# Conditioned linear attention: two bias sums in column groups, another bank for one key product, and another order of the first loads

## The reference

```python
xn = _ln(x, ln_w, ln_b)
q = xn @ Wq + bq
k = xn @ Wk + bk + (1.0 - src_mask) * -1000000.0
q = softmax(q.reshape(b, t, h, dh), axis=-1)      # h = 8 heads of dh = 64
k = softmax(k.reshape(b, t, h, dh), axis=1)       # over the tokens
v = ((xn @ Wv + bv) * src_mask).reshape(b, t, h, dh)
att = einsum('bnhd,bnhl->bhdl', k, v)
y = einsum('bnhd,bhdl->bnhl', q, att).reshape(b, t, d)
scale, shift = split(silu(emb) @ W_emb + b_emb)
hh = _ln(y, ln2_w, ln2_b) * (1.0 + scale) + shift
return x + silu(hh) @ W_out + b_out
```

## Time and profile before

| | us |
|---|---|
| median of 3 runs | 471.26 (470.62 to 471.79) |
| the profiled execution | 471.46 |
| its span, first to last instruction | 469.5 |
| PE busy | 459.6 (98%) |
| DVE busy | 347.2 (74%) |
| ACT busy | 255.7 (54%) |
| POOL busy | 133.8 (28%) |

### The profile page before, as it was taken

How to read it: one execution, slowest core, us unless ns; L and a number is a source line. 1 busy time by engine, 2 the same in 40 slices (tenths; PEclk the granted TensorE clock), 3 DMA queues, 4 the chain that set the end, 5 groups by cost and what they waited for, 6 DMA issues and landing times.

```text
span 469.5 us, 7280 instructions
## 1 busy us (share of the span) xinstructions
PE 459.6 (98%) x2486; PEld 375.0 (80%) x2486; DVE 347.2 (74%) x844; ACT 255.7 (54%) x471; POOL 133.8 (28%) x149
## 2 busy tenths in 40 slices
PE   4999999999999999999999999999999999999997
PEld 3678877886888878888888888888878868888886
DVE  6768947776987947879768667676999827886852
ACT  5524322331878533347655555566799923766771
POOL 0413310221110000104323222225300032786685
PEclk9999999999999999999999999999999999999999
DMA  7936401111233201110212130312232032343322
GB/s 268 379 115 238 167 2 46 45 45 57 100 100 112 96 9 45 47 45 1 67 46 90 53 113 18 134 66 72 98 108 88 0 109 73 114 134 114 112 91 89
DMA packets 23187, 43.49 MB, mean 93 GB/s; under 512 B 1960, under 2 KB 2288, under 8 KB 23152
## 3 DMA queue, kind: packets, MB, share of 16 engines
q1 hardware_dynamic: 22592, 41.98, 26.0%
q10 hardware_dynamic: 560, 1.05, 0.6%
HBM read 34.64 MB, written 8.39 MB: 92 GB/s over the span
## 4 chain that ended last, share of the span: by engine, by line
PE 97%; DVE 1%; DMA 1%; ACT 0%; issue 0%; DVEq 0%
PE ps L1237 25%; PE ps L1239 25%; PE ps L1238 25%; PE ps L1242 10%; PE ps L1419 6%; PE ps L1341 2%; PE ps L1305 1%; PE ps L1397 1%; PE ps L1313 1%; PE ps L1262 1%; PE ps L1297 1%; DMA x_in<-in_x_dram 1%; PE ps L1401 0%; PE ps L1320 0%; ACT x_in L352 0%
## 5 line engine op out<-in xcount | busy, mean ns | idle before, releaser
L623 POOL TENSOR_TENSOR qs<-qs,qmax 128x512 f32<-128x512 f32 x32 | 36.1, 1130 | 172.0 <-DVE qmax L829 172.0
L1237 PE MATMUL ps<-wq_hi,zT_hi 128*128 128x512 f32 x128 | 52.2, 408 | 0.0
L1237 PE MATMUL ps<-wk_hi,zT_hi 128*128 128x512 f32 x124 | 51.1, 412 | 1.0 <-DVE kf L810 1.0
L338 ACT ACTIVATE zT_hi<-ps 128x512 fp32r<-128x512 f32 x32 | 19.1, 596 | 60.0 <-PE ps L1242 60.0
L1237 PE MATMUL ps<-ek_hi,zm_hi 128*128 128x512 f32 x128 | 50.4, 393 | 0.0
L1239 PE MATMUL ps<-wq_hi,zT_lo 128*128 128x512 f32 x128 | 50.2, 392 | 0.0
L1238 PE MATMUL ps<-wq_lo,zT_hi 128*128 128x512 f32 x128 | 49.9, 390 | 0.0
L1239 PE MATMUL ps<-ek_hi,zm_lo 128*128 128x512 f32 x128 | 49.9, 390 | 0.0
L1238 PE MATMUL ps<-ek_lo,zm_hi 128*128 128x512 f32 x128 | 49.8, 389 | 0.0
L1239 PE MATMUL ps<-wk_hi,zT_lo 128*128 128x512 f32 x124 | 48.7, 393 | 0.0
L1238 PE MATMUL ps<-wk_lo,zT_hi 128*128 128x512 f32 x124 | 48.3, 390 | 0.0
(11 more groups left out here) (250 smaller groups left out, 1156.8 us busy)
## 6 DMA issues: line engine op xcount, KB each, us to landing
x_in<-in_x_dram SPq DMA_DIRECT2D x35, 512.0 KB, 3.6
res<-in_x_dram SPq DMA_DIRECT2D x24, 256.0 KB, 2.8
out_dram<-res SPq DMA_DIRECT2D x24, 256.0 KB, 2.0
out_dram<-x_in SPq DMA_DIRECT2D x7, 256.0 KB, 2.0
y<-in_L_cond_Wk_dram ACTq DMA_DIRECT2D x2, 512.0 KB, 4.4
kf<-in_L_cond_Wq_dram SPq DMA_DIRECT2D x1, 1024.0 KB, 6.3
eq<-in_L_cond_W_out_dram SPq DMA_DIRECT2D x1, 1024.0 KB, 8.3
wv_mod<-in_L_cond_Wv_dram SPq DMA_DIRECT2D x1, 1024.0 KB, 10.5
```

The lines of the kernel that those rows point to most:

```text
L338: act.activation(o, i, ACT.Copy, scale=scale).then_inc(s[done], 1)
L623: pool.tensor_tensor(q_heads, q_heads, qmax[:, n % 2, :].unsqueeze(2).broadcast_to([P, H, DH]), ALU.subtract).then_inc(s["q_shift"], 1)
L1237: pe.matmul(o, a[0], bb[0], start=start, stop=False)
```

## The change

Three edits. The bias sums of query and value are formed as four matmuls with 32 columns of weights, each into its own 32 partitions of bank YTB, one per block (`bias_parts`); ScalarE copies that bank to `bias_part` in SBUF; one full matmul with `part`, a 128x128 matrix of 1/32, sums the parts and spreads them on all partitions (`bias_sum`), into bank YB + 1. The query's parts are formed ahead of `product_q(0, 0)` and summed behind it, the value's are formed in step 7 and summed in step 8. The key product of tile 15 of the first batch goes to bank OB, and the state's first products in banks 0 and 3 wait for all 16 key sums. ScalarE requests the first half of wk ahead of ln_w and ln_b.

```diff
-        bv_all = kf[:, 14, :]
+        bias_part, bv_all = kf[:, 15, :], kf[:, 14, :]
...
+            def load_wk(half):
+                act.dma_start(wk_raw[:, 2 * half:2 * half + 2, :],
+                              wk.rearrange("(c p) n -> p c n", p=P)[:, 2 * half:2 * half + 2, :]).then_inc(s[f"wk_in{half}"], 16)
+
+            load_wk(0)
             for v, at in ((ln_w, LNW), (ln_b, LNB)):
                 act.dma_start(ln_rows[at:at + NB, :], v.rearrange("(c p) -> c p", p=P)).then_inc(s["ln_in"], 16)
-            for half in range(2):
-                act.dma_start(wk_raw[:, 2 * half:2 * half + 2, :],
-                              wk.rearrange("(c p) n -> p c n", p=P)[:, 2 * half:2 * half + 2, :]).then_inc(s[f"wk_in{half}"], 16)
+            load_wk(1)
...
                 copy(wq_scaled[:, f, :], wq_raw[:, f, :], "wq_scaled", ln_weight(f))
+            act.wait_ge(s["bq_part"], 1)
+            copy(bias_part, ps[:, YTB, :], "bq_copy")
             normalise_x(0, 2)
             normalise_x(0, 3)
             for n in range(T):
                 if 2 <= n + 1 < T:
                     zT_high(0, n + 1)
+                if n == 8:
+                    act.wait_ge(s["bv_part"], 1)
+                    copy(bias_part, ps[:, YTB, :], "bv_copy")
...
-                dve.scalar_tensor_tensor(out=kf[:, n, :], in0=ps[:, OB if m == 1 else KB, :], scalar=pen[:, m:m + 1],
+                dve.scalar_tensor_tensor(out=kf[:, n, :], in0=ps[:, OB if m in (1, T - 1) else KB, :], scalar=pen[:, m:m + 1],
...
-            dve.tensor_tensor(bq_all[:], bq_all[:], ps[:, YTB, :], ALU.add).then_inc(s["bq_ok"], 1)
+            dve.tensor_tensor(bq_all[:], bq_all[:], ps[:, YB + 1, :], ALU.add).then_inc(s["bq_ok"], 1)
...
-                if m >= 2:
+                if m == T - 1:
+                    pe.wait_ge(s["k_sum"], 2)
+                elif m >= 2:
                     pe.wait_ge(s["k_sum"], m if m > 2 else 1)
...
-            def bias_sum(bank, by, raw, done):
+            def bias_parts(bank, by, raw, done):
 
                 for f in range(NB):
-                    last = pe.matmul(ps[:, bank, :], by[:, f:f + 1].broadcast_to([P, P]), raw[:, f, :],
-                                     start=(f == 0), stop=(f == NB - 1))
+                    last = pe.matmul(ps[32 * f:32 * f + 32, bank, :], by[:, f:f + 1].broadcast_to([P, 32]), raw[:, f, :],
+                                     start=True, stop=True)
                 last.then_inc(s[done], 1)
+
+            def bias_sum(bank, parts, done):
+                pe.matmul(ps[:, bank, :], part[:], parts, start=True, stop=True).then_inc(s[done], 1)
...
+                    if n == 0 and j in (0, 3) and b == 0:
+
+                        pe.wait_ge(s["k_sum"], T)
...
             pe.wait_ge(s["wq_in"], 16)
+            bias_parts(YTB, cols[:, LNB:LNB + NB], wq_raw, "bq_part")
             product_q(0, 0)
-            bias_sum(YTB, cols[:, LNB:LNB + NB], wq_raw, "bq_ps")
+            pe.wait_ge(s["bq_copy"], 1)
+            pe.wait_ge(s["part_ok"], 1)
+            pe.wait_ge(s["cols_ok"], 2)
+            bias_sum(YB + 1, bias_part, "bq_ps")
...
                     pe.wait_ge(s["wv_in"], 16)
-                    pe.wait_ge(s["cols_ok"], 2)
-                    bias_sum(YB + 1, lnb_w, wv_mod, "bv_ps")
+                    bias_parts(YTB, lnb_w, wv_mod, "bv_part")
+                if n == 8:
+                    pe.wait_ge(s["bv_copy"], 1)
+                    bias_sum(YB + 1, bias_part, "bv_ps")
```

More of the change, by code:

```diff
@@ L204, in cond_linear_attention @@
         names = """table_ok ln_in vec_in wk_in0 wk_in1 wq_in wv_in wo_in bk_in bq_in bias_in ident0 ident_ok part_ok ones_ok pick_ok
-            vec_ps cols_ok lnbw_ok kb_ps bq_ps bv_ps bk_ok bq_ok row_ok
+            vec_ps cols_ok lnbw_ok kb_ps bq_part bq_copy bq_ps bv_part bv_copy bv_ps bk_ok bq_ok row_ok
             wk_hi_ok wk_lo_ok wq_hi_ok wq_scaled wq_lo_ok wv_ok wo_hi_ok wo_lo_ok
@@ L1271, in product_k @@
                 for f in range(NB if m else 0):
-                    last = split_product(ps[:, OB if m == 1 else KB, :], (zT_hi[:, n % 2, f, :], zT_lo[:, n % 2, f, :]),
+                    last = split_product(ps[:, OB if m in (1, T - 1) else KB, :], (zT_hi[:, n % 2, f, :], zT_lo[:, n % 2, f, :]),
                                          (wk_hi[:, f, :], wk_lo[:, f, :]), f == 0, f == NB - 1)
```

## The result

| | before | changed kernel |
|---|---|---|
| median of timed runs | 471.94 us (470.62 to 472.29, 6 runs) | 468.38 us (467.78 to 469.00, 6 runs) |
| profiled execution | 471.46 us, span 469.5 | 469.00 us, span 467.0 |
| ratio | | 0.9929 (95%: 0.9914 to 0.9944) |

The change makes the kernel 3.35 us faster (2.6 to 4.1 by the interval); 468.3 had been forecast. The span of the profiled execution fell by 2.5 us, a little less than the timed runs.

The account below looks back on a forecast made before the run. TensorE's own work, 97% of the span, was taken to bound the kernel. Bias sums -2.84, key -1.2 and first loads +1.1 gave -2.95 us, so 468.3 us from a median of 471.26, range 466.6 to 470.4.

Parts of the forecast that it names:

- Part 1: Query and value bias sums in TensorE's queue: 2.01 us each in place of 3.43, gaining 2.84 us for both.
- 1.15 or 0.93 for one round: Cost in us of one four-group round: 1.15 with the switch paid once, 0.93 as half of 1.85; 1.15 was taken.
- Both copies: ScalarE's copies of the query's and value's bias parts: costed at nothing, about 0.9 us each without cover.
- Rival C: Bias sums: the four column groups do not run beside each other; 2.2 us slower, 473.5 us; 4%.
- Part 2: Last key product of the first batch: TensorE's wait for VectorE's key sum goes, gaining 1.2 us (0.8 to 1.25).
- Rival D: The key's hole only moves, to the maximum's transposes or the state's first product; -1.75 us, 469.5 us; 9%.
- Part 3: Order of first loads: half of wk put ahead delays the second x tile or layernorm rows; 1.1 us lost (0 to 1.4).
- What the start waits for is not wk: At the start, the chain runs from x tiles through statistics, VectorE's short steps and normalisation to TensorE at 8.19 us.
- Nothing pays for it: At the start, no gain offsets the 1.1 us loss: ScalarE's wk scaling already ends early, TensorE does not wait for wq.
- Rival A: At the start, the reordered load costs nothing or little; -4.0 us, 467.2 us; 15%.
- The clock: Step in matmul spacing from 0.43 to 0.23 us: moves with the later start (loss 1.1) or stays (0.55); 1.1 kept.
- rival B: Later start also lets the clock's step slip by up to 3.4 us, costing another 1.6 us; 469.9 us; 12%.

Follow-up runs that it names:

- e4: Changed kernel with the old load order and the last key product back in its old bank, so bias sums in groups alone; 468.62 us, ratio 0.9932.
- e7: Changed kernel with the old load order and the value's four 32-column matmuls done five times over instead of once; 469.89 us, one run.
- e3: Kernel before with only the last key product of the first batch moved to the output's bank, plus the needed waits; 470.84 us, ratio 0.998.
- e2: Kernel before with only the new order of ScalarE's first loads; 472.70 us, ratio 1.0015.
- e1: Changed kernel with ScalarE's old load order, layernorm rows and then both halves of wk; 467.55 us, ratio 0.9912.
- e8: The changed kernel measured again, with nothing altered, for a second sample of its start; 468.35 us, ratio 0.9936.
- e12: Changed kernel with the old load order, measured a second time; 468.21 us, ratio 0.992.
- e6: Changed kernel with the first half of wk requested between ln_w and ln_b, the second half after them; 468.19 us, ratio 0.9928.
- e10: Changed kernel with the old load order and the second half of wk requested only when the first has landed; 470.75 us, ratio 0.9977.
- e9: Changed kernel with the old load order, the key's bias also in column groups and two key sums moved later on VectorE; 468.11 us, ratio 0.9929.

## Why the prediction was right

**Part 1, the sums: right.** 1.15 for a round, 0.86 for the full matmul, 1.42 gained per sum; the traces have 1.15, 0.86, 1.42 and 1.35, and e4 alone has 2.81 for both in place of 2.84. The step that could have gone wrong, 1.15 or 0.93 for one round, was decided by e7: the 0.29 for the switch comes once. Both copies were costed at nothing, and TensorE waits for neither; the normalisations ended 1.6 us ahead of their transposes, where about 2 were forecast. One bound was off: with the switch doubled a sum gains 3.43 - 1.44 - 0.86 = 1.13, not 1.2. Rival C (groups one behind another) is false: eight instructions start within 1.06 us.

**Part 2, the key: right.** 1.2 forecast, 1.17 at the hole in the profiled pair, 1.33 in e3 with the small steps behind it. Rival D (the hole moves) is false: nothing is idle behind it, the second conditioning product is still 1.85, and the gain stands at the state's first product in full.

**Part 3, the start: sign and path right, size by luck.** As predicted, the half of wk requested first goes through ahead of the second x tile; the two statistics are split, the copy of the columns is late, the transposes are late. Against the one trace that the prediction had, the loss is 1.5 us, not 1.1: of the 1.35 us that 512 KB need at 387 GB/s, 0.25 were taken off for idle engine time, and nothing more was moved in it (272 GB/s in that microsecond). Against the timed runs it is 0.7 (e2, 0.1 to 1.3) to 0.8 (changed kernel against e1, which is a difference of two ratios, whose intervals reach 0.7 and 0.9 us to either side; e8 against e12 gives the same). The step that failed is the one that said what the start waits for: "What the start waits for is not wk", and "Nothing pays for it". It was read off one execution, and in that one the half of wk landed 3.8 us after its request. In the five other traces of the old order it took 4.5 to 6.0, and then the key bias, which stands ahead of the transposes in TensorE's queue, waits for it and sets the start. The wait stood in the trace of before, 1.7 us long, and the prediction passed over it where it called 3.6 and 1.0 the longest waits; it was short enough for x to be later by 0.6. The new order removes that wait, and pays for part of what it costs by that. The forecast of 1.1 lies between an error down and an error up. Rival A (no cost at all) is excluded by e2's interval, if barely.

The prediction also left open in what order the loads of two queues go. The changed kernel's trace shows it:

```profile
q10 hardware_dynamic: 184, 0.38, 99.3%
q1 hardware_dynamic: 11, 0.00, 1.6%
```

**The clock: the step moved with the work in the profiled pair, the reason for more is open.** The changed kernel's rows against the earlier trace rows:

```profile
14.22 0.63 PE L1270 MATMUL ps<-wk_hi,zT_hi 128*128 128x512 f32 x1
14.64 0.63 PE L1270 MATMUL ps<-wk_lo,zT_hi 128*128 128x512 f32 x1
...
16.12 0.39 PE L1245 MATMUL ps<-wk_hi,zT_hi 128*128 128x512 f32 x1
16.35 0.40 PE L1246 MATMUL ps<-wk_lo,zT_hi 128*128 128x512 f32 x1
```

From the transposes to tile 1's product are 6.43 us, 6.40 before: no slip in that pair, so rival B did not happen against the trace it was written from. The two spacings, 0.43 and 0.23, are the levels of 1.2 and 2.4 GHz. Over all traces, though, the new order has 6.17 to 6.59, and the old order 5.33 to 5.58 in the five traces where the key bias runs straight into the transposes. There the closer spacing comes 1.1 to 3.8 us behind the start of the transposes, in the new order 5.1 to 6.0 (in the trace of before 5.6); in e1 it is there from 11.83:

```profile
11.83 0.39 PE L1270 MATMUL ps<-wk_hi,zT_hi 128*128 128x512 f32 x1
12.06 0.40 PE L1270 MATMUL ps<-wk_lo,zT_hi 128*128 128x512 f32 x1
```

It would be natural to say that the unbroken stretch brings the clock up sooner, and that the new order, with a gap of 1.24 ahead of the transposes, loses some of that. But e6 has a gap of 1.08 there and still 5.39. So this was not shown, and the 0.8 us by which the distance differs between most traces stays open: against the other traces of the old order something like rival B did happen.

At tile 1's product the traces of the two orders differ by 1.36 (16.00 against 14.64), the timed runs by 0.7 to 0.8. Part of that is which executions have a trace. Both traces of the changed kernel are of the slowest execution of their set (469.00 with a median of 468.38, and 469.04 with 468.35), those of e1 and e12 are 0.3 below the median and at it.

**The best version** is probably the one without Part 3 (e1: 0.9912, and again 0.992), 0.8 us ahead of the changed kernel; the intervals (0.9893 to 0.9931 and 0.9914 to 0.9944) overlap, and what separates them is e2, whose interval excludes no change.

## What to carry to other kernels

Count a sum inside a full queue from start to start of its neighbours, take off what stands there anyway, and keep a fixed cost (here 0.29 us for the switch to narrow weights and back) apart from the one per round: then such a forecast can hold to hundredths, as it did here. Where a start hangs on several loads that land close together, one execution does not say which is last: look at each wait, ask how far the next late one is behind, and give that edit the widest bounds. Before a load is put ahead of others, ask which loads it passes and which small ones stand behind it in its own queue, since both paid for its length in full here.

## What had not been expected of the hardware

- The same 512 KB load, requested at 1.58 us in the same place, took from 3.8 to 6.0 us over six traces. All other loads around it were the same; the engines moved 387 to 184 GB/s in the window of 4 to 5 us.
- Loads of two queues went whole, one behind another, and not side by side: half of wk requested at 0.71 ran between the two x tiles, requested just behind the second one it ran after both. And a load is as late as its last engine: in e6 one closing packet of 16 came 0.85 us behind the other 15, in e10 two.
- Putting more requests ahead raised the throughput of the third microsecond not at all (289 to 272 GB/s; 304 in e1, in the old order), though 15% of the engines' time had been idle there.
- The granted clock reads 1.00 in the early windows in which matmuls of one shape start 0.43 us apart, and equally in those in which they start 0.23 apart, so early in a kernel the spacing has to be read. Later it can show: after 2.17 us without a matmul (e10) the spacing was back at 0.43 to 0.50, and the granted clock read 0.50.
- One execution of e9 took 1360.66 us, the four others of the same kernel 467.35 to 468.16. Its matmuls started 0.5 to 0.84 us apart all along, and its granted clock read 1.00.
